# The 128x128 transposes of a gated linear-scan and ternary feed-forward kernel go from TensorE to transposing DMAs, and the quantization of one token tile is put into the matmul loop of the next

## The reference, cut to what matters

```python
xn = layernorm(x)                                   # over 1024 features, per token
g, v, d = xn @ Wg + bg, xn @ Wv + bv, xn @ Wd + bd  # 1024 -> 1024 each
h_t = a_t * h_{t-1} + sigmoid(g_t) * tanh(v_t)      # over tokens, a = 0.001 + 0.998*sigmoid(d)
xq  = round(xn * 127/max|xn|)                       # per token, whole numbers
wq  = clip(round(w / mean|w|), -1, 1)               # for w_gate, w_up (1024 -> 4096), w_down
p   = silu(xq @ wq_gate) * (xq @ wq_up)             # with the scales, 4096 per token
out = x + h + (round(p * 127/max|p|) @ wq_down)     # max over the 4096 of the token
```

## Time and profile before

| | |
|---|---|
| median of 3 runs | 6459.69 us (6456.21 to 6482.13) |
| the profiled execution, its own time | 6456.43 us |
| its span on the slowest core (core 5) | 6454.1 us (6424.6 to 6454.1 over the cores) |
| busy on core 5 | PE 2244.3 us (35%), DVE 3104.0 us (48%), ACT 740.2 us (11%) |
| DMA | 420.49 MB, mean 65 GB/s |

### The profile page before, as it was taken

The page is one execution under the profiler, slowest core; times in us unless marked ns, Lnnn a source line. Parts: engine busy times, 40 slices in busy tenths (PEclk is TensorE's granted clock), DMA queues, the critical chain, the costliest instruction groups (busy, mean ns, idle before and its releaser), DMA issues.

```text
span 6454.1 us, 46275 instructions; the slowest of 8 cores (6424.6 to 6454.1 us)
## 1 busy us (share of the span) xinstructions
PE 2244.3 (35%) x11794; PEld 1185.1 (18%) x11794; DVE 3104.0 (48%) x5413; ACT 740.2 (11%) x1252; POOL 16.2 (0%) x34
## 2 busy tenths in 40 slices
PE   0044334333110111342444244424442444256655
PEld 0033333222000000111111111111111111122222
DVE  2344554555565666555545554555455545511111
ACT  0122221111010111111111111111110111000000
POOL 1000000000000000000000000000000000000000
PEclk9976666666555555566666666666666666677777
DMA  4210000000425232100000000000000000077777
GB/s 85 65 33 33 26 28 33 32 31 33 140 69 166 76 124 77 38 17 17 9 17 17 17 8 17 17 17 9 17 17 17 8 17 17 28 256 252 247 241 241
DMA packets 206656, 420.49 MB, mean 65 GB/s; under 512 B 55808, under 2 KB 72224, under 8 KB 198208
## 3 DMA queue, kind: packets, MB, share of 16 engines
q1 hardware_dynamic: 202752, 411.13, 19.7%
q0 software_dynamic: 3648, 6.41, 0.6%
HBM read 339.86 MB, written 83.89 MB: 66 GB/s over the span
## 4 chain that ended last, share of the span: by engine, by line
DVE 44%; PE 27%; DMA 9%; issue 8%; ACT 4%; SPq 4%; DVEq 2%; POOL 0%; ACTq 0%; POOLq 0%
PE pb L576 8%; PE pb L580 7%; PE pb L680 7%; DVE qt L194 4%; DVE qg L206 3%; DVE qnd L204 3%; DVE qt L208 3%; DVE qnd L209 3%; DVE pqroll L210 3%; DMA wqg<-scr_wdT 3%; DVE qg L451 2%; PE pb L380 2%; DVE scal L600 2%; DVE qcm L203 2%; DVE qci L202 2%
## 5 line engine op out<-in xcount | busy, mean ns | idle before, releaser
L576 PE MATMUL pb<-wqg,xqF_t 128*128 128x512 bf16 x2048 | 827.2, 404 | 249.8 <-DMA xqF_t<-scr_xqF 249.8
L580 PE MATMUL pb<-wqu,xqF_t 128*128 128x512 bf16 x2048 | 824.4, 403 | 0.0
L225 PE MATMUL ptb<-idb_sb,pqroll 128*128 128x128 bf16 x1024 | 149.7, 300 | 1573.6 <-DVE pqroll L210 1573.6
L680 PE MATMUL pb<-wqg 128*128 128x512 bf16 x2048 | 481.7, 400 | 328.3 <-DMA wqg<-scr_wdT 328.2
L595 DVE SCALAR_TENSOR_TENSOR pbuf<-pb,dvecs,epi 128x512 f32<-128x512 f32 x128 | 96.1, 751 | 702.1 <-ACT epi L590 702.1
L380 PE MATMUL pb<-wqu,wqg 128*128 128x256 bf16 x3072 | 400.6, 294 | 16.3 <-ACT wqu L229 16.3
L698 DVE TENSOR_SCALAR qt<-pb,dpwall 128x512 f32<-128x512 f32 x64 | 48.0, 751 | 718.2 <-PE pb L680 704.3
L225 PEld LDWEIGHTS ptb<-idb_sb,pqroll 128*128 128x128 bf16 x1024 | 88.9, 126 | 1641.7 <-issue 1641.7
L225 PE MATMUL ptb<-idb_sb,pqstage 128*128 128x128 bf16 x1024 | 146.0, 302 | 670.7 <-DVE pqstage L200 631.2
L225 PE MATMUL ptb<-idb_sb,wqu 128*128 128x128 bf16 x256 | 34.9, 303 | 961.5 <-DVE pqstage L210 952.4
L229 ACT ACTIVATE pqstage<-ptb 128x512 bf16<-128x512 bf16 x256 | 153.0, 598 | 1565.7 <-PE ptb L225 1565.7
(11 more groups left out here) (88 smaller groups left out, 2567.8 us busy)
## 6 DMA issues: line engine op xcount, KB each, us to landing
wqg<-scr_wdT SPq DMA_DIRECT2D x512, 256.0 KB, 4.0
pbuf<-wdown SPq DMA_DIRECT2D x64, 512.0 KB, 4.5
pbuf<-wgate SPq DMA_DIRECT2D x64, 512.0 KB, 4.1
pbuf<-wup SPq DMA_DIRECT2D x64, 512.0 KB, 4.1
scr_pqF<-pqstage SPq DMA_DIRECT2D x32, 1024.0 KB, 4.1
wqg<-scr_pqF SPq DMA_DIRECT2D x32, 1024.0 KB, 7.8
pbuf<-x SPq DMA_DIRECT2D x32, 512.0 KB, 3.7
x_grp<-x SPq DMA_DIRECT2D x32, 512.0 KB, 4.7
```

Of the source, the lines that this page charges most:

```text
L225: e.transpose(o, i_, idb[:]),
L576: e.matmul(o, l, r, start=st, stop=sp),
L580: e.matmul(o, l, r, start=st, stop=sp),
L680: e.matmul(o, l, r, start=st, stop=sp),
```

## The change

1. `emit_transpose4` becomes `emit_xpose4`: each of its four blocks is moved by a `dma_start_transpose` from SBUF to SBUF, written into SyncE's list. Eight semaphores (`TD0` to `TD7`) are used in turn, a call waits for the call eight before it, and those who used the result of ScalarE or TensorE now wait for the last eight calls.
2. In the tile stage the rounding and transposing of tile i-1 is written into the slab loop of tile i: in slab s the transposes of piece s-2 are issued, and VectorE rounds piece s of tile i-1 just before it writes slab s of tile i over it. Pieces 6 and 7, and the store, come after the slab loop. The last tile is drained after the loop. The roll has four slots instead of two (`qtmp` gives two more).
3. The `nop`s that held VectorE and ScalarE until the store of the tile before had landed are gone; the first transpose into `pqstage` waits for that store instead.

```diff
-        def emit_transpose4(srcs, dst_ap, src_wait=(), dst_wait=()):
+        def emit_xpose4(srcs, dst_ap, src_wait=(), extra_wait=()):
             n = tp_state["n"]
             tp_state["n"] += 1
-            bank = n % 2
...
+            sem = TD[n % 8]
+            twait = list(src_wait) + list(extra_wait)
+            if n - 8 >= 0:
+                twait.append(tp_state["marks"][n - 8])
             for i, s4 in enumerate(srcs):
-                op("t", lambda e, i_=s4, o=ptb[bank][:, (base + i) * 128:(base + i + 1) * 128]:
-                   e.transpose(o, i_, idb[:]),
...
+                op("y", lambda e, i_=s4, o=dst_ap[:, i * 128:(i + 1) * 128]:
+                   e.dma_start_transpose(o, i_),
+                   sem=sem, inc=16, wait=tuple(twait) if i == 0 else ())
+            tp_state["marks"].append(wv(sem))
...
-            xn_evac_marks = (wv(V), wv(S))
+            xn_evac_marks = xpose_marks_g
...
-                tmark_prev_batch = wv(T)
+                tmark_prev_batch = last_xpose_marks(8)
...
+        roll = [pqroll[:, 0:512], pqroll[:, 512:1024], qtmp[:, 0:512], qtmp[:, 512:1024]]
...
+        def b1_quant_piece(ti, pc):
+            slot = roll[pc % 4]
+            pw = []
+            if (ti, pc) in roll_reader:
+                pw.append(roll_reader[(ti, pc)])
+            emit_round_neg(pbuf[:, pc * 512:(pc + 1) * 512], scal[:, 1:2], slot,
+                           pre_wait=tuple(pw))
+
+        def b1_xpose_piece(ti, pc, extra=()):
+            slot = roll[pc % 4]
+            emit_xpose4([slot[:, b4 * 128:(b4 + 1) * 128] for b4 in range(4)],
+                        pqstage[:, pc * 512:(pc + 1) * 512],
+                        src_wait=(wv(V),), extra_wait=extra)
...
+        def b1_store(ti):
+            marks = tuple(b1_piece_marks[(ti, pc)] for pc in range(8))
+            op("y", lambda e, i_=pqstage, o=scr_pqF[ti]:
+               e.dma_start(out=o, in_=i_[:]), sem=SP, inc=16, wait=marks)
...
-            if i > 0:
-                op("v", lambda e: e.nop(), wait=((SP, st_pq[i - 1]),))
-                op("s", lambda e: e.nop(), wait=((SP, st_pq[i - 1]),))
...
                 silu_mark = wv(S)
                 bank_marks[bkg] = silu_mark
+                if i > 0:
+                    if s_ >= 2:
...
+                        b1_xpose_piece(i - 1, s_ - 2, extra=ex)
+                    b1_quant_piece(i - 1, s_)
                 op("v", lambda e, i_=pu_, o=pbuf[:, s_ * 512:(s_ + 1) * 512], sc=dvecs[:, 1:2],
...
+            t_after_tile[i] = T.n
+            if i > 0:
+                b1_xpose_piece(i - 1, 6)
+                b1_xpose_piece(i - 1, 7)
+                b1_store(i - 1)
...
-            for pc in range(8):
-                dst_roll = pqroll[:, (pc % 2) * 512:(pc % 2) * 512 + 512]
...
+        i = NT - 1
+        for pc in range(8):
+            b1_quant_piece(i, pc)
+            if pc >= 2:
+                b1_xpose_piece(i, pc - 2,
+                               extra=((SP, st_pq[NT - 2]),) if pc == 2 else ())
+        b1_xpose_piece(i, 6)
+        b1_xpose_piece(i, 7)
+        b1_store(i)
```

More of the change, by code:

```diff
@@ L139, in build_program @@
                  "LP2", "LP3", "LW4", "LW5", "LW6", "LW7",
+                 "TD0", "TD1", "TD2", "TD3", "TD4", "TD5", "TD6", "TD7",
                  "SA", "SX", "SW", "SP", "SO0", "SO1"]
@@ L152, in build_program @@
         SO = [sems["SO0"], sems["SO1"]]
+        TD = [sems[f"TD{j}"] for j in range(8)]
         block = es.enter_context(nc.Block())
@@ L212, in build_program, with last_xpose_marks @@
         tp_state = {"n": 0, "marks": []}
-        def emit_transpose4(srcs, dst_ap, src_wait=(), dst_wait=()):
+        def emit_xpose4(srcs, dst_ap, src_wait=(), extra_wait=()):
             n = tp_state["n"]
             tp_state["n"] += 1
-            bank = n % 2
[L218 to L222, removed]
-            for i, s4 in enumerate(srcs):
-                op("t", lambda e, i_=s4, o=ptb[bank][:, (base + i) * 128:(base + i + 1) * 128]:
-                   e.transpose(o, i_, idb[:]),
[L226 to L231, removed]
+            sem = TD[n % 8]
+            twait = list(src_wait) + list(extra_wait)
+            if n - 8 >= 0:
+                twait.append(tp_state["marks"][n - 8])
+            for i, s4 in enumerate(srcs):
+                op("y", lambda e, i_=s4, o=dst_ap[:, i * 128:(i + 1) * 128]:
+                   e.dma_start_transpose(o, i_),
+                   sem=sem, inc=16, wait=tuple(twait) if i == 0 else ())
+            tp_state["marks"].append(wv(sem))
+        def last_xpose_marks(k=8):
+            return tuple(tp_state["marks"][-k:]) if tp_state["marks"] else ()
         for dst, src in ((consts_sb, d_consts), (idf, d_idf), (idb, d_idb),
@@ L278, in build_program @@
         act_marks = [None, None]
-        xpose_mark = None
+        xpose_marks_g = None
         xg_read_done = {}
@@ L299, in build_program @@
                 ln_wait = [ld_x]
-                if xpose_mark is not None and tt == 0:
-                    ln_wait.append(xpose_mark)
+                if xpose_marks_g is not None and tt == 0:
+                    ln_wait.extend(xpose_marks_g)
                 op("v", lambda e, i_=xtile, o=xnb, m=meanall[:, idx:idx + 1],
@@ L314, in build_program @@
                 for pc in range(2):
-                    qw = (xpose_mark,) if (xpose_mark is not None and tt == 0 and pc == 0) else ()
+                    qw = xpose_marks_g if (xpose_marks_g is not None and tt == 0 and pc == 0) else ()
                     emit_round_neg(xnb[:, pc * 512:(pc + 1) * 512], sv,
@@ L321, in build_program @@
                 k = 2 * kp
-                emit_transpose4(
+                emit_xpose4(
                     [xnbf(0 * D + k * 128, 128), xnbf(1 * D + k * 128, 128),
@@ L333, in build_program @@
                     xqF(k * GRP, 512), src_wait=srcw)
-            xpose_mark = wv(T)
-            xn_evac_marks = (wv(V), wv(S))
+            xpose_marks_g = last_xpose_marks(8)
+            xn_evac_marks = xpose_marks_g
             sd_mark = None
@@ L409, in build_program @@
             emit_acc_dma(1)
-            v_done, s_done = wv(V), wv(S)
             for k in range(8):
@@ L414, in build_program @@
                    e.dma_start(out=o, in_=i_), sem=SX, inc=16,
-                   wait=(s_done, v_done) if k == 0 else ())
+                   wait=xpose_marks_g if k == 0 else ())
             sa_group[g] = SA.n
@@ L460, in prep_quant @@
             vmarks = {}
-            tmark_prev_batch = None
+            tmark_prev_batch = last_xpose_marks(8)
             for bi in range(len(load_list) // 4):
@@ L473, in prep_quant @@
                         pw = [ldw] if pc == 0 else []
-                        if pc == 0 and tmark_prev_batch is not None:
-                            pw.append(tmark_prev_batch)
+                        if pc == 0 and tmark_prev_batch:
+                            pw.extend(tmark_prev_batch)
                         if li == 0:
@@ L499, in down_dest4 @@
             kglob = q * 8 + kb
-            emit_transpose4([qtmp4(cc, kb * 128, 128) for cc in range(4)],
-                            wdT_build(kglob * D + c0 * 128, 512), src_wait=srcw)
+            emit_xpose4([qtmp4(cc, kb * 128, 128) for cc in range(4)],
+                        wdT_build(kglob * D + c0 * 128, 512), src_wait=srcw)
         prep_quant(down_l2, 4, down_dest4)
-        v_done, s_done = wv(V), wv(S)
+        dmarks = last_xpose_marks(8)
         for k in range(32):
@@ L506, in build_program @@
                e.dma_start(out=o, in_=i_), sem=SW, inc=16,
-               wait=(v_done, s_done) if k == 0 else ())
+               wait=dmarks if k == 0 else ())
         st_wdT = SW.n
@@ L516, in gate_dest4 @@
             c0 = metas[0]
-            emit_transpose4([qtmp4(cc, kb * 128, 128) for cc in range(4)],
-                            wqg[:, kb * INNER + c0 * 128: kb * INNER + c0 * 128 + 512],
-                            src_wait=srcw)
+            emit_xpose4([qtmp4(cc, kb * 128, 128) for cc in range(4)],
+                        wqg[:, kb * INNER + c0 * 128: kb * INNER + c0 * 128 + 512],
+                        src_wait=srcw)
         prep_quant(gate_l2, 0, gate_dest4)
@@ L528, in up_dest4 @@
             c0 = metas[0]
-            emit_transpose4([qtmp4(cc, kb * 128, 128) for cc in range(4)],
-                            wqu[:, kb * INNER + c0 * 128: kb * INNER + c0 * 128 + 512],
-                            src_wait=srcw)
+            emit_xpose4([qtmp4(cc, kb * 128, 128) for cc in range(4)],
+                        wqu[:, kb * INNER + c0 * 128: kb * INNER + c0 * 128 + 512],
+                        src_wait=srcw)
         prep_quant(up_l2, 2, up_dest4, pre_first=((SW, st_wdT),))
@@ L537, in build_program @@
         bank_marks = [None] * 6
-        roll_marks = []
         sg2_marks = [None, None]
+        prep_w_marks = last_xpose_marks(8)
+        roll = [pqroll[:, 0:512], pqroll[:, 512:1024], qtmp[:, 0:512], qtmp[:, 512:1024]]
```

(28 more changed lines are left out.)

## The result

The changed kernel takes 7347.53 us (median of 8 runs, 7343.95 to 7353.72) against 6459.31 us for the kernel before (8 runs beside it): 1.137 times as long, 95% interval 1.1355 to 1.1384. The forecast was 7250 us, with a chance of 0.84 for slower.

A forecast was written before the change was run, and what follows sets the result against it. VectorE was taken to lead outside the DMA-heavy down projection, the rest being hand-over with TensorE. Scan +533, weight +873 and tile -611 us sum to +795 on 6456.4 us: forecast 7250 us, range 6500 to 8540.

The forecast's parts named there:

- c: Microseconds SyncE's list and the DMA rings need per transposing DMA of a 128x128 block in a row; taken as 1.2.
- the sum: Change of all three stages together: 1536c - 1048, +795 us at c = 1.2, breaking even at c = 0.68.
- Scan stage: 16 groups, each with 32 uncovered transposes and a landing before its matmuls: 512c - 81, +533 us at c = 1.2.
- Weight stage: 24 batches, next batch's loads stand behind 32 transposes and VectorE waits: 768c - 49, +873 us at c = 1.2.
- Tile stage: Rounding overlaps the next tile's slabs, eight transposes stay at each border: 256c - 918, -611 us at c = 1.2.
- Rival 1: Transposing DMAs paced like plain loads, c = 0.45 to 0.60, so the overlap wins: 6099 to 6330 us; chance 0.12.
- Rival 2: Each transpose lands before the next moves, c = 1.9, and SyncE's list bounds the tile: 8534 us; chance 0.2.
- Rival 3: TensorE's clock stays low in the tile stage, matmuls 0.43 us apart: +74 us, 7325; chance inside the forecast's 0.65.

The follow-up runs named there:

- experiment 5: The changed kernel with each 128x128 block in the tile stage moved as two transposing DMAs of 64x128: 8388.3 us.
- experiment 3: The changed kernel with wider transposing DMAs, 128x1024 in scan and weight stages and 128x512 in the tile stage: 5744.3 us, 0.887 of the kernel before.
- experiment 4: The changed kernel with each transposing DMA replaced by a plain DMA of the same 128x128 block, transposition left out: 6396.5 us.
- experiment 6: The changed kernel with the eight loads of the next tile issued in slab 1 instead of behind the store: 6950.7 us.
- the overlap alone: The changed kernel with transposes back on TensorE and copies on ScalarE, rounding kept in the next tile's slab loop: 5601.7 us, 0.865 of the kernel before.
- experiment 2: The changed kernel without the overlap: transposing DMAs everywhere, each tile rounded after its own eight slabs: 8080.7 us.
- experiment 8: experiment 3 with next-tile loads in slab 1, each wide DMA issued once its source is rounded, and finer waits: 5582.7 us, 0.863 of the kernel before.
- experiment 9: experiment 8 with the weight-stage loads written four ahead of their use: 5062.6 us, 0.783 of the kernel before.

## Why the prediction was right

The forecast rested on one unknown, c, and on counting where each transpose lies. Step by step:

- **c = 1.2** was the middle between two far ends and is 1.27 in the trace. That is 1536 x 0.07 = +107 us, more than the whole difference of 98 us between forecast and result. With 1.27 the sum gives 7359. As a choice it was luck as much as argument: my reason for it (the scatter of 2-byte elements costs) does not hold. Halving the bytes of an instruction changes its time on the list by 0.01 us, and octupling them by 0.08 to 0.16 us in rows of four (experiments 5 and 3), so the price is nearly all the instruction's, twice that of a plain copy of one block (experiment 4). The sum did not notice, since every instruction here held one block.
- **Scan stage**: 512c - 81 = +569 at 1.27; measured +575. As predicted, nothing covers the 32 transposes.
- **Weight stage**: 768c - 49 = +926; measured +947. As predicted, the load behind the transposes is what ends VectorE's wait, and it comes after 4.4 us where I had 4.1. But the loads' place in the list is only a small part of the loss. The last transpose lands at about 3132.7 by my estimate (3131.48, and the 1.2 us that the tile border shows), and the rounding waits for it too. So with early loads VectorE would still have stood some 42 of its 45.4 us, and the loads' place costs about 3.3 us a batch, 80 in all. No run of this kernel has only those loads moved.
- **Tile stage**: 256c - 918 = -593; measured -628. A tile is 71.7 us against 72.7: the last transpose lands about 1.2 us after its issue has ended (5098.95 to 5100.17), not 1.9, since over half of the 2.3 us from issue to landing is the issue itself; and the first slab took 5.93 us (5035.79 to 5041.72) instead of 6.46. The place of the loss is shown by experiment 6: moving the loads alone gives 397 us back.
- **Rival 1** (paced like plain DMAs) is what experiment 4 measured, without the transposition. The Trainium skill, Advanced Engine Details and Errata, section "X-Bar Transpose (TRN2)", has transposing DMAs as fast as regular ones; the trace disagrees for blocks of this size, 1.27 us against 0.62. The Trainium skill, VectorE: DVE Perf Modes, section "The three transpose paths", gives 1309 ns for such a block, and the 1.27 us of the trace agree with it.
- **Rival 2** (each lands before the next moves) did not happen: they land 2.3 us after issue and follow each other by 1.27. Its other half, the list as the bound of a tile, was built in experiment 5 and came out at its formula.
- **Rival 3** (low clock in the tile stage) did not either: the stage's granted clock rose from 0.65 to 0.74, and products kept 6.49 us. Its working names the wrong pair of rows: the two starts there are 0.38 us apart, and 0.43 is the spacing of the matmuls that follow them.

Gain and loss can each be had without the other, but they don't simply add: the overlap alone is 868 us faster, the DMAs alone 1611 us slower, which would make 743, and both together are 888 us slower. The rest is the border of the tile (experiment 2). What stays open is what the 1.27 us per instruction consist of. Two things speak for the issuing side rather than for the DMA engines. Transposes in a row of 32 still land 2.3 us after their issue, so no work piles up behind them. And in such a row (2121.2 to 2162.2) the 16 DMA engines are busy 12% in the mean and move 25 GB/s, while in a row of four 128x1024 (2219.8 to 2225.4 of experiment 3) they are busy 77% and move 147 GB/s. Which step of the issuing takes the time, no run shows.

## What to carry to other kernels

Before moving small operations to a DMA queue, multiply their number by the time of one issue, and then list what stands behind them in that queue: here most of the loss was paid where the matmuls of the scan stage and the next rounding of the weight stage waited for rows of 32 transposes. Loads that should run ahead belong in front of what waits for computing: that order alone was worth 520 us between experiments 8 and 9, and 397 us in experiment 6. If a DMA must be issued often, make each one larger: 416 wide instructions did the same work for 1600 us less. And an overlap and a new engine for a part of it are two edits; tried one at a time, the first was a gain of 13.5% by itself.

## What the runs showed of the hardware

A transposing DMA from SBUF to SBUF (bf16) occupied SyncE's list for 1.26 to 1.28 us at 64x128, 1.25 to 1.29 us at 128x128 and 1.25 us at 128x512 (2.50 us for two). At 128x1024 it was 1.24 us when issued singly (experiment 9) and 1.35 to 1.43 us in rows of four (experiment 3). I had expected its time to grow with its bytes. 256 KB in 1.35 us are 194 GB/s. A plain copy of 128x128 took 0.62 us there. The Trainium skill, DMA: Bandwidth & Descriptors, section "Rules for kernel authors", advises to coalesce transfers under 64 KB; these rows show it for transposes.
